# The matrix of edge counts of a four-layer graph network: plain scatters of counts that VectorE works out, in place of accumulating scatters of ones

## The reference

```python
x = _layernorm(x + _L0_gnn_ref(x, edge_index, ...))   # attention in both directions
x = _layernorm(x + _L1_gnn_ref(x, ..., node_type_3, edge_index, edge_type_4))  # two HGT attention layers
x = _layernorm(x + _L2_gnn_ref(x, edge_index, L2_gnn_W, L2_gnn_b))   # segment_sum(h[src] * norm, dst)
x = _layernorm(x + _L3_gnn_ref(x, edge_index, edge_weight1, ...))    # mean over dst of x[src] + edge term
```

## Time and profile before

| | us |
|---|---|
| median of 3 runs (9284.9 to 9291.43) | 9291.03 |
| the profiled execution | 9288.31 |
| its span, first to last instruction | 9286.2 |
| POOL busy | 5776.8 |
| DVE busy | 4982.0 |

### The profile page before, as it was taken

How to read it: one execution, slowest core, us unless ns; L and a number is a source line. 1 busy time by engine, 2 the same in 40 slices (tenths; PEclk the granted TensorE clock), 3 DMA queues, 4 the chain that set the end, 5 groups by cost and what they waited for, 6 DMA issues and landing times. The chain is left out here.

```text
span 9286.2 us, 65164 instructions
## 1 busy us (share of the span) xinstructions
PE 2819.9 (30%) x19883; PEld 2216.5 (24%) x19883; DVE 4982.0 (54%) x8546; ACT 2921.4 (31%) x3159; POOL 5776.8 (62%) x5419
## 2 busy tenths in 40 slices
PE   5666635555100005400000000270000000059997
PEld 5666525555100005300000000160000000034443
DVE  7555547766699996444444444434444446740212
ACT  6333313333366662222222222232222223410001
POOL 2777777777777767677777777657777777610000
PEclk8555555555555557755555555585555555569998
DMA  5655224444466655444444434453444445546653
GB/s 140 212 197 191 82 72 143 130 135 133 152 217 217 219 198 155 134 109 111 111 110 111 110 103 111 112 156 98 110 111 111 111 111 159 182 72 192 196 189 115
DMA packets 576000, 1306.03 MB, mean 141 GB/s; under 512 B 249724, under 2 KB 344654, under 8 KB 521766
## 3 DMA queue, kind: packets, MB, share of 16 engines
q1 hardware_dynamic: 252742, 889.07, 28.3%
q0 software_dynamic: 292960, 358.27, 16.7%
q10 hardware_dynamic: 29952, 54.54, 2.4%
HBM read 782.92 MB, written 518.52 MB: 140 GB/s over the span
## 5 line engine op out<-in xcount | busy, mean ns | idle before, releaser
L1465 POOL DMA_INDIRECT l_swp_G<-table,KVI x1664 | 1605.2, 965 | 512.5 <-issue 327.1
L1410 POOL DMA_INDIRECT adj<-ONE,CELL x832 | 1344.2, 1616 | 728.0 <-DMA adj<-ONE,CELL 486.7
L1586 DVE TENSOR_TENSOR l_swp_PROD<-l_swp_G,l_swp_QS 128x1024 f32<-128x1024 f32 x208 | 253.9, 1221 | 2005.5 <-DMA l_swp_G<-table,KVI 2005.4
L1691 PE MATMUL l_swp_AW<-l_swp_ET,ones 128*128 128x512 f32 x4 | 4.2, 1141 | 3932.3 <-DVE l_swp_ET L1669 3932.3
L1110 POOL DMA_INDIRECT arrived<-plc_QS,plc_idx x832 | 814.1, 979 | 253.6 <-issue 245.4
L1110 POOL DMA_INDIRECT slots<-REC,plc_idx x832 | 796.9, 958 | 273.4 <-issue 252.8
L1522 ACT ACTIVATE l_swp_VT<-l_swp_G 128x2048 f32<-128x2048 f32 x104 | 385.8, 3710 | 1826.6 <-issue 1692.4
L1195 POOL DMA_INDIRECT l_G<-table,OTHI x832 | 786.2, 945 | 256.1 <-issue 252.9
L1691 PEld LDWEIGHTS l_swp_AW<-l_swp_ET,ones 128*128 128x128 f32 x4 | 1.0, 312 | 3932.6 <-DVE l_swp_ET L1669 3932.6
L949 PE MATMUL plc_pr<-plc_seen,plc_otf 128*128 128x49 f32 x3328 | 861.6, 414 | 12.8 <-DVE plc_seen L698 12.8
L949 PEld LDWEIGHTS plc_pr<-plc_seen,plc_otf 128*128 128x128 f32 x3328 | 846.8, 326 | 32.4 <-issue 32.1
(11 more groups left out here) (502 smaller groups left out, 8294.6 us busy)
## 6 DMA issues: line engine op xcount, KB each, us to landing
sums<-l_ROW SPq DMA_DIRECT2D x104, 1088.0 KB, 4.7
l_swp_QX<-queries SPq DMA_DIRECT2D x104, 1088.0 KB, 7.8
dn_AR<-adj SPq DMA_DIRECT2D x100, 832.0 KB, 4.6
adj<-plc_zrow SPq DMA_DIRECT2D x100, 800.0 KB
dn_AR<-adj SPq DMA_DIRECT2D x100, 768.0 KB, 4.3
queries<-plc_zrow SPq DMA_DIRECT2D x55, 1088.0 KB
sums<-l_swp_ROW SPq DMA_DIRECT2D x52, 1096.0 KB, 5.5
plc_QX<-queries SPq DMA_DIRECT2D x104, 544.0 KB, 4.4
```

The source lines that it names most:

```text
L1410: pool.indirect_dma_start(out=g.cells, out_offset=bass.IndirectOffsetOnAxis(ap=g.CELL[:, g.put:g.put + 1], axis=0), in_=g.ONE[:, 0:1], in_ ...
L1465: pool.indirect_dma_start(out=G[:, c % GR, j, :], out_offset=None, in_=table, in_offset=bass.IndirectOffsetOnAxis(ap=index[:, c * CK + j:c ...
```

## The change

**The scatter.** `put_cell` loses `compute_op=ALU.add` and the wait on `g.landed`. It now writes a count from `VAL` and waits once in eight calls, for `g.celled`, until VectorE has made these eight columns' counts.

**The counts.** In `plc0`, eight more parts of `table_part` (chunks 12 to 19) make `KEY` (the number of the node's segment in the row, times 8192, plus the other node: equal keys are equal edges) and `AGAIN` (1 where an equal key stands earlier in the same group of eight columns). In each chunk c of the attention sweeps VectorE handles one group of eight columns: `later`, eight times, compares one key with all keys behind it and sums the hits; `cells` finds the first place of each of the eight keys, writes `VAL` = 1 + hits, and sends every entry that is not the first of its kind to a spare row of `adj`.

**The places.** The first sweep handles groups 0 to 51, the second 52 to 103. POOL scatters from chunk 5 on (`BEHIND` = 5), one after every second gather, with 16 behind the gathers and 8 behind the gather of `FR`. "t0" has none, "t1" the 16 that are left of the first half, "t2" the last 16.

```diff
-EVERY = 2
+BEHIND = 5
...
-def put_cell(pool, passed, g):
-    if g.put < EC:
-        if g.put:
-            pool.wait_ge(g.landed, 16 * g.put)
+def put_cell(pool, passed, g, upto):
+    if g.put < upto * 8:
+        if g.put % 8 == 0:
+            pool.wait_ge(g.celled, g.put // 8 + 1)
             passed()
...
-                                in_=g.ONE[:, 0:1], in_offset=None, compute_op=ALU.add).then_inc(g.landed, 16)
+                                in_=g.VAL[:, g.put:g.put + 1], in_offset=None).then_inc(g.landed, 16)
...
+                elif i == 11:
+                    link(v.tensor_tensor_scan(t[:, :], F[:, :], F[:, :], 0.0, ALU.add, ALU.max))
+                    link(v.scalar_tensor_tensor(out=g.KEY[:, :], in0=t[:, :], scalar=float(1 << SHIFT), in1=g.OTHI[:, :],
+                                                op0=ALU.mult, op1=ALU.add))
+                    link(v.memset(g.AGAIN[:, :, :], 0.0))
...
+                elif i < 19:
...
+                    link(v.tensor_tensor(same, key[:, :, d:8], key[:, :, 0:8 - d], ALU.is_equal))
+                    link(v.tensor_tensor(g.AGAIN[:, :, d:8], g.AGAIN[:, :, d:8], same, ALU.max))
...
-                    if j % EVERY == EVERY - 1:
-                        put_cell(pool, passed, g)
-            for _ in range(8):
-                put_cell(pool, passed, g)
+                    if c >= BEHIND and j % 2 == 1:
+                        put_cell(pool, passed, g, (part + 1) * NCK)
+            for _ in range(16):
+                put_cell(pool, passed, g, (part + 1) * NCK)
...
+            def later(c, i):
+                q = part * NCK + c
+                x = q * 8 + i
+                if i >= 2:
+                    v.wait_ge(told, pick.n + i - 1)
...
+                    v.tensor_scalar(EQ[:, x % 2, 0:EC - 1 - x], g.KEY[:, x + 1:EC], g.KEY[:, x:x + 1], 0.0, ALU.is_equal, ALU.add,
+                                    accum_out=RPT[:, i:i + 1]).then_inc(told, 1)
+
+            def cells(c):
...
+                v.max_index(FIND[:, :], g.KEY[:, at], g.KEY[:, 0:q * 8 + 8]).then_inc(told, 1)
+                pick.n += 9
+                v.wait_ge(told, pick.n)
+                v.tensor_scalar(g.VAL[:, at], RPT[:, :], 1.0, None, ALU.add)
+                pick(v.scalar_tensor_tensor(out=DROP[:, 0, :], in0=FIND[:, :], scalar=float(-q * 8), in1=g.iota[:, 0:8],
+                                            op0=ALU.add, op1=ALU.not_equal))
+                v.tensor_tensor(DROP[:, 1, :], DROP[:, 0, :], g.AGAIN[:, q, :], ALU.max)
+                pick(v.tensor_scalar(AWAY[:, :], g.iota[:, 0:8], g.SPARE[:, 0:1], float(q * 8), ALU.add, ALU.add))
+                pick(v.copy_predicated(g.CELL[:, at], DROP[:, 1, :], AWAY[:, :]))
+                v.sem_inc(g.celled, 1)
...
+                    if c >= 0 and x % 2 == 1:
+                        later(c, x // 2)
...
+                if c >= 0:
+                    cells(c)
...
                     if n >= AHEAD * GT - 1:
                         put_query(n - AHEAD * GT + 1)
-                        put_cell(pool, passed, g)
...
-                    if gcn and n % 3 == 2:
-                        put_cell(pool, passed, g)
```

33 lines of the change are left out of this document (27 added, 6 removed).

## The result

The changed kernel takes 8396.64 us (median of 4 runs, 8387.73 to 8399.31) where the kernel before, on the same chip, takes 9288.21 (4 runs): a ratio of 0.9038, 95% interval 0.9023 to 0.9054. The forecast was 8466 with a range from 8420 to 8640.

The account below looks back on a forecast made before the run. It took POOL, with its gathers, adds and waits for landings, to pace both attention sweeps. Terms -774 + 4 - 64 + 10 = -824 us from 9288.3 gave 8464, with the median 2.7 above: 8466 us, range 8420 to 8640.

Parts of the forecast that it names:

- Part 1: Gathers and scatters in the sweeps: each sweep's gathers take 1533 us, gaining 516 and 258 us, 774 together.
- rival of the dear plain scatter: A plain scatter with different columns might cost the add's 1.62 us: +481 us, 8945; chance 0.04.
- VectorE beside it: In the sweeps, VectorE's mean chunk takes 26.9 and 24.0 us against POOL's 30.5, so the counts cost nothing.
- rival of 2.15 ns an element: VectorE becomes the bound in the first sweep if comparisons run at the scan's rate: +171 us, 8635; chance 0.10.
- cover of 134 and 285: Time in us that VectorE has free beside POOL in the first and second sweep; what exceeds it is paid in full.
- Part 2: The sweeps' ends: the first about equal (-1), the second longer by 5, together +4 us.
- Part 3: The two `turn_layer`s: with adds gone from "t0" and mostly "t1", TensorE's waits shrink, -40 and -24 us.
- TensorE may take over part: In "t0" and "t1", the reason for taking -40 and -24 us, below the upper bounds of 45 and 29.
- Part 4: What is added elsewhere: +5 us for VectorE's new instructions holding up POOL in `plc0`, +5 for `cells`.
- factor of 0.77: Share of a VectorE instruction's length by which it holds POOL up, from (2.25 - 0.965) / 1.67.
- second rival: The comparisons hold POOL for 0.77 of their length in the sweeps: 423 us on top, about 8870; chance 0.07.
- something that I don't see: Last item of the chances: an unseen effect, on the fast side of before; chance 0.02.

Follow-up runs that it names:

- e3: The changed kernel with only the accumulate operation put back into its scatters, without the wait for landings; 8914.13 us.
- e17: The changed kernel with each comparison of `later` made three times in all; 8820.29 us where the kernel before takes 9288, ratios 1.0023 to 1.0047 on slower chips.
- e4: The changed kernel without any counting (`later`, `cells` and the new table parts left out, counts a constant 1, addresses all different); 8390.04 us.
- e5: The changed kernel with each comparison of `later` made a second time, into a place nobody reads; 8494.12 us.
- e1: The kernel before with the adds of "t0" and "t1" moved to the free places of the second sweep; 9434.81 us.
- e2: The changed kernel with one additional plain scatter of a constant word behind each query of "t0" and "t1" (98 in all); 8423.38 us.
- e8: The kernel before with six more matmuls for each of tiles 1 to 28 of "t0", ahead of TensorE's wait for `t_qr`; 9300.49 us, ratio 1.0006.
- e6: The changed kernel with the comparison written as an instruction that reads two f32 inputs from SBUF, also with a sum; 8467.95 us.

## Why the prediction was right, and where it was wrong

**Part 1** was right in each term, and its phases came out by their terms and not by luck: the pattern on the timeline is the one in the sum. A plain scatter is 0.98 us between gathers, chunks take 30.5 from the sixth on, and the phases came to 1530.6 and 1531.2 where 1533 was forecast. e3 confirms the division into length and wait. The rival of the dear plain scatter is out: 832 of them have a mean of 992 ns.

**VectorE beside it** was right in its verdict, and too high in its numbers. The comparisons measure 1070 ns at 831 elements and 645 in the middle, near my line through the earlier trace rows (1.07 and 0.66), and about 210 at the end (0.25), so the rival of 2.15 ns an element is out. But adding up durations overstates an engine's load: see e17. VectorE still waited 239 us for gathers in the first sweep and 394 in the second, where I had a cover of 134 and 285, and it caught up by the tenth chunk and not the fifteenth. It didn't matter for the forecast, since VectorE had room either way (e4: less than 1 us in each phase), but it made the expectation for e5 miss by 158 us.

**Part 2**, +4, measured -7. The first end had adds in it before, of 1.61 us and with waits, and those go: 46.6 with adds (e1), 39.9 with plain scatters, 36.6 without counts (e4). I had forecast the counts' cost there (2 to 5 us, measured 3.3 and 1.9) and offset it against too small a gain. At the second end the counts' 1.9 us are met by 2.3 that the end got shorter (39.1 to 36.8 in e4), which I had not seen: where gathers come every 1.25 us, as in the last quarter before, VectorE may be further behind when they end. That reason wasn't tested.

**Part 3 is the step that failed**, by 35 us: -64 forecast, -98.6 measured. It read the price of the adds off TensorE's recorded waits on `t_qr` and POOL's lag at the end, 45 and 29 us, and called these upper bounds. They were none, because the stage didn't end with TensorE. POOL's own queue filled both stages: it waited for queries 8.5 us in "t0" and never in "t1", and spent 34.1 and 76.7 us waiting for landings of adds. No row on POOL's waits in these stages was read. From POOL's first query to the fetch of `t_first` it is 263.9 us before and 201.7 after in "t0", 223.5 and 186.7 in "t1", which is all that was gained. e1 shows that nothing but the adds is in it, and e2 that POOL's time per tile counts: 22 x (5.73 - 4.05) = 37 us in "t0" and 13 at its end are 50 of the 62, and the landing waits, which come on top, weren't separated.

Seen from TensorE, "t0" lost 27.0 us of waits on `t_qr`, 7.8 of waits for `X`, 13.0 from TensorE's last matmul to the first gather (23.2 to 10.2), and 16.1 of TensorE's busy time; "t1" lost 15.5, 11.7 at the end (21.7 to 10.1) and 10.7 of busy time. The busy time is what the bounds left out: behind a stall TensorE ran at the lower clock level, so its delay by POOL was recorded partly as waiting and partly as slower work. That it was no cost beside POOL's follows from POOL's waits, not from e8. I also took -40 and -24, below even my bounds, for a "TensorE may take over part" that no row supported.

**Part 4**, +10, measured nothing: up to "t0" -1.6 in place of +5, and no trace of `cells` in the phases. The factor of 0.77 from one pair of rows was the mistake of the second rival, and half of the table's work the same kind of guess. One scatter of 2.25 us beside one instruction of 1.67 says how long a hold-up can be, not how often there is one (the median of the 49 in its group is 0.96); e6 gives a share of an eighth over 831 instructions. By it, an estimate, 10 us of such work cost about 1. The Trainium skill ("SBUF — State Buffer", "Who interferes with whom") speaks of a pair of ports that one of the two engines holds for the whole instruction, and says that two inputs contend with GpSimd's reads and the summing `tensor_scalar` doesn't. The runs agree in direction for both forms (two inputs slow POOL's DMAs, the summing `tensor_scalar` leaves their time alone, 954 ns with it and without), but for DMAs issued by POOL the price is this small one.

**"t2" and the dense layers** gave 6.9 us that no term had. In ten comparable profiles this stretch is 1209.9 to 1212.2 us with adds (four kernels) and 1203.7 to 1208.1 with the changed kernel's plain scatters (six). The two groups don't overlap, but adds stand in this stretch in one of the four only, and by what path adds could lengthen it isn't shown.

**The sum**: 35 of the 69 us in part 3, 11 in the ends, 12 in the costs of part 4, 7 behind the sweeps, 5 in the gather phases. All of them point the same way, since each bound on a cost was taken on the dear side and each on a gain on the small side. The spread of 25 us for parts 3 and 4 was too small even for part 3 alone, and the range reached only 46 us below the forecast against 174 above it: a time below 8420 fell to the last item of the chances, "something that I don't see", with 0.02. (The terms as written add up to 8467, not 8466.)

## What to carry to other kernels

An engine that waits for another shows only part of its delay as waiting; the rest hides in work done slowly behind the stall. So first look which engine never waits for the other, and size the stall by the two engines' time per step, not by the recorded waits of the one that stalls. Load an engine from start to start of its instructions, not by their durations. And before spending VectorE's idle time, ask what happens when its own pace drops a little: on the slower chips the version with the most on VectorE lost its whole gain.
